# State-space tiles: one decay matrix for both directions, time steps in the scans, the gate on GpSimd

## The reference

```python
def segsum_exp(a):   # out[..., i, j] = exp(sum_{k=j+1..i} a[..., k]) for i >= j, else 0
...
Lmat = segsum_exp(A)
Y_diag = jnp.einsum('bcln,bcsn,bhcls,bcshp->bclhp', C, B, Lmat, x)     # x is xh * dt
decay_states = jnp.exp(A_cs[..., -1:] - A_cs)
states = jnp.einsum('bcln,bhcl,bclhp->bchpn', B, decay_states, x)
...
Y_off = jnp.einsum('bcln,bchpn,bhcl->bclhp', C, states, jnp.exp(A_cs))
Y = (Y_diag + Y_off).reshape(b, L, h, p)
...
y = jnp.concatenate([jnp.zeros_like(y[:, :1]), y[:, :-1]], axis=1)
y_fw, y_bw = (y[:b], jnp.flip(y[b:], 1))
fd = x_og @ fc_D_w.T + D
y = y_fw + y_bw + x_og * jnp.repeat(fd, HEADDIM, axis=-1)
yg = y * silu(z)
yn = yg * jax.lax.rsqrt(jnp.mean(yg * yg, axis=-1, keepdims=True) + EPS) * norm_w
return yn @ out_proj_w.T
```

## Time and profile before

| what | us |
|---|---|
| median of 3 runs | 2144.38 (2143.53 to 2150.88) |
| the profiled execution, device time | 2126.43 |
| its span | 2124.7 |
| TensorE busy | 1811.0 (85%) |
| VectorE busy | 1494.5 (70%) |
| ScalarE busy | 1003.0 (47%) |
| GpSimd busy | 447.5 (21%) |

### The profile page before, as it was taken

How to read it: one execution, slowest core, us unless ns; L and a number is a source line. 1 busy time by engine, 2 the same in 40 slices (tenths; PEclk the granted TensorE clock), 3 DMA queues, 4 the chain that set the end, 5 groups by cost and what they waited for, 6 DMA issues and landing times. The chain is left out here.

```text
span 2124.7 us, 33254 instructions
## 1 busy us (share of the span) xinstructions
PE 1811.0 (85%) x10026; PEld 1240.0 (58%) x10026; DVE 1494.5 (70%) x3126; ACT 1003.0 (47%) x2291; POOL 447.5 (21%) x411
## 2 busy tenths in 40 slices
PE   5288898898898969999945695899999898989897
PEld 2146656666666559999942253464656465646564
DVE  5668878788788761222236696878887879888885
ACT  2032242241331412212202254878797979787886
POOL 2113413314314232522111202020111102020101
PEclk9589999899898989999977797999999999999998
DMA  4501221221122119755445294143443424343311
GB/s 161 181 32 60 88 70 59 77 81 59 59 70 88 50 68 320 257 187 179 139 131 175 75 300 135 51 101 69 100 89 86 95 68 102 81 90 80 80 31 31
DMA packets 143788, 226.09 MB, mean 106 GB/s; under 512 B 17725, under 2 KB 110015, under 8 KB 143648
## 3 DMA queue, kind: packets, MB, share of 16 engines
q1 hardware_dynamic: 124464, 179.95, 27.6%
q0 software_dynamic: 19184, 44.45, 8.3%
HBM read 174.26 MB, written 50.99 MB: 106 GB/s over the span
## 5 line engine op out<-in xcount | busy, mean ns | idle before, releaser
L2239 DVE TENSOR_SCALAR att_scores<-att_psS 128x512 f32<-128x512 f32 x512 | 348.7, 681 | 74.7 <-PE att_psS L2073 60.0
L2188 ACT ACTIVATE att_prob<-att_scores,att_shift 128x512 f32<-128x512 f32 x512 | 383.3, 749 | 30.3 <-DVE att_shift L2255 30.3
L2197 ACT COPY att_pT<-att_psT 128x512 f32<-128x512 f32 x512 | 305.7, 598 | 140.3 <-PE att_psT L2081 139.9
L2081 PEld LDWEIGHTS att_psT<-ident,att_prob 128*128 128x128 f32 x2048 | 244.7, 142 | 176.9 <-issue 78.4
L2247 DVE CUSTOM_DVE_ANT_0 att_scores<-att_scores,first_decay 128x512 f32<-128x512 f32 x512 | 347.6, 679 | 0.0
L2081 PE MATMUL att_psT<-ident,att_prob 128*128 128x128 f32 x2048 | 317.0, 278 | 26.6 <-ACT att_pT L2197 26.0
L2073 PE MATMUL att_psS<-first_ks,first_qs 128*128 128x512 bf16 x512 | 197.5, 387 | 33.5 <-DVE att_scores L2239 29.4
L2095 PE MATMUL att_psO<-att_pT,att_v 128*32 128x512 f32 x1024 | 139.6, 620 | 24.5 <-ACT att_pT L2197 24.5
L1233 DVE TENSOR_TENSOR_SCAN mamba_L<-mamba_am,mamba_begin 128x1024 f32<-128x1024 f32 x64 | 145.5, 2295 | 15.0 <-PE mamba_psY L954 14.7
L1460 PEld LDWEIGHTS ffn_psH<-ffn_xT,ffn_w 128*128 128x128 f32 x1248 | 147.3, 194 | 3.6 <-issue 1.7
L1460 PE MATMUL ffn_psH<-ffn_xT,ffn_w 128*128 128x128 f32 x1248 | 147.7, 277 | 1.1 <-ACT ffn_xT L1494 1.1
(11 more groups left out here) (282 smaller groups left out, 2916.7 us busy)
## 6 DMA issues: line engine op xcount, KB each, us to landing
ffn_w<-in_w SPq DMA_DIRECT2D x39, 1024.0 KB, 5.1
mamba_am<-a_rows SPq DMA_DIRECT2D x64, 512.0 KB, 3.7
first_qs<-q_parts SPq DMA_DIRECT2D x256, 64.0 KB
first_ks<-k_parts SPq DMA_DIRECT2D x256, 64.0 KB
xn<-xn_all SPq DMA_DIRECT2D x16, 512.0 KB, 5.8
ffn_w<-in_w POOLq DMA_DIRECT2D x8, 1024.0 KB, 6.2
att_w<-in_inter POOLq DMA_DIRECT2D x7, 1024.0 KB, 6.1
att_w<-in_outer POOLq DMA_DIRECT2D x7, 1024.0 KB, 7.2
```

The source lines that it names most:

```text
L2081: mm = nc.tensor.transpose(ps[:, k * P:(k + 1) * P], prob[:, n % NP, k * P:(k + 1) * P], C.ident[:])
L2188: nc.scalar.activation(prob[:, n % NP], scores[:, n % NCL], ACT.Exp, bias=shift[:, h % 2, t:t + 1], accum_out=total[:, octet % 2, t, j, i: ...
L2197: nc.scalar.copy(pT[:, h % HEADS_T, :, t * P:(t + 1) * P], bank_of("turn", n)[:].rearrange("p (k q) -> p k q", k=CPB)).then_inc(pT_ready, 1)
L2239: vec.tensor_scalar(scores[:, n % NCL], psS[n % NS][:], -CLAMP, CLAMP, ALU.max, ALU.min).then_inc(clipped, 1)
```

## The change

In the third part the two directions of a tile share one matrix. A scan's `begin` now holds the time step of the row's token and direction instead of 1, so that `xdt` isn't needed and the diagonal product takes `xl` itself. Since the forward matrix is 0 above the diagonal of the shifted tile and the backward one below, GpSimd adds the two (`join`), VectorE picks for every place the product of its direction (`choose`: by masks `side`, then a sum of both halves into `pair`), multiplies once per tile (`decays`), and TensorE's diagonal product runs once per tile. `begin` is made anew for each unit by a select of GpSimd (`beginnings`) in the memory of the table's `hot_row`, four buffers. The gate's multiplication moves from VectorE's `finish` to GpSimd (`gate`). Four scans instead of three stand ahead of `dtdec`, and VectorE's and TensorE's loops go over tiles instead of units. The diff, cut to its core (the declarations, semaphores and renamed counts of waits are left out):

```diff
-    NA, NL = 4, 3
+    NA, NM, NB = 4, 3, 4
...
+        begin = table.hot_row[:].rearrange("p k (b h) t -> p (k b) h t", b=NB)
... (TensorE)
-                    def diagonal(u):
-                        t, d = u // 2, u % 2
-                        if d == 0:
...
-                        pe.wait_ge(L_ready, i * U + u + 1)
-                        pe.wait_ge(xdt_ready, i * U + u + 1)
+                    def diagonal(t):
...
+                        pe.wait_ge(L_ready, i * CPB + t + 1)
                         for h in range(NH):
-                            mm = nc.tensor.matmul(psY[:, h * HD:(h + 1) * HD], L[:, u % NL, h], xdt[:, u % 2, h * HD:(h + 1) * HD],
+                            mm = nc.tensor.matmul(psY[:, h * HD:(h + 1) * HD], fwd[:, t % NM, h], xl[:, t, h * HD:(h + 1) * HD],
...
+                    def from_states(t):
+                        for d in range(2):
+                            if (d == 0 and t > 0) or (d == 1 and t < CPB - 1):
+                                pe.wait_ge(state_ready, (i + 1) * 6)
+                                done = [2 * (t - 1) if t > 1 else 0, 2 * t][d]
+                                pe.wait_ge(off_scaled, i * 6 + done)
...
-                    diagonal(0)
-                    for u in range(2, U + 1):
-                        if u % 2 == 0 and 4 <= u < U:
-                            products(u // 2)
-                        diagonal(u - 1)
-                        if u in (4, 6):
-                            turn_tile(u // 2 - 2)
-                            output(u // 2 - 2)
+                    for t in range(CPB):
+                        diagonal(t)
+                        from_states(t)
+                        if t + 2 < CPB:
+                            products(t + 2)
+                        if 1 <= t < CPB - 1:
+                            turn_tile(t - 1)
+                            output(t - 1)
... (GpSimd)
+                    def beginnings(t):
+                        pool.wait_ge(decayed, i * U + max(2 * t + 2 - NB, 0))
+                        nc.gpsimd.tensor_tensor(turn[:, t:t + 1], C.ones[:, 0:1], C.ones[:, 0:1], ALU.mult)
+                        for d in range(2):
+                            u = 2 * t + d
+                            side_of = 1 - 2 * d
+                            nc.gpsimd.affine_select(out=begin[:, u % NB], in_=dtb[:, d, t].unsqueeze(2).to_broadcast([P, NH, P]),
+                                                    compare_op=ALU.is_equal, fill=0.0, base=-1,
+                                                    pattern=[[0, NH], [side_of, P]], channel_multiplier=-side_of).then_inc(begin_ready, 1)
+                    def gate(t):
+                        pool.wait_ge(z_ready, (i + 1) * CPB)
+                        pool.wait_ge(summed, i * CPB + t + 1)
+                        nc.gpsimd.tensor_tensor(y[:, t % 2], y[:, t % 2], zs[:, t], ALU.mult).then_inc(gated, 1)
+                    def join(t):
+                        pool.wait_ge(decayed, i * U + 2 * t + 2)
+                        nc.gpsimd.tensor_tensor(fwd[:, t % NM], fwd[:, t % NM], bwd[:, t % 2], ALU.add).then_inc(joined, 1)
+                    pool.wait_ge(ab_ready, i + 1)
+                    beginnings(0)
+                    beginnings(1)
+                    join(0)
... (VectorE)
+                    def choose(t):
+                        dve.wait_ge(g_ready, i * CPB + t + 1)
+                        v.tensor_tensor(masked[:], gT[t % 2], side[:], ALU.mult).then_inc(sided, 1)
+                        dve.wait_ge(sided, i * CPB + t + 1)
+                        c.step(v.tensor_tensor(pair[:, t % 2], masked[:, 0], masked[:, 1], ALU.add))
+                    def decays(t):
+                        dve.wait_ge(joined, i * CPB + t + 1)
+                        v.tensor_tensor(fwd[:, t % NM], fwd[:, t % NM], pair[:, t % 2].unsqueeze(1).to_broadcast([P, NH, P]), ALU.mult).then_inc(L_ready, 1)
...
-                        dve.wait_ge(summed, i * CPB + t + 1)
-                        v.tensor_tensor(y[:, b], y[:, b], zs[:, t], ALU.mult).then_inc(gated, 1)
...
+                    choose(0)
                     decays(0)
                     grow(0)
-                    decays(1)
+                    choose(1)
                     grow(1)
                     grow(2)
+                    decays(1)
...
+                    for t in range(CPB):
+                        if 1 <= t and t + 1 < CPB:
+                            choose(t + 1)
+                            decays(t + 1)
+                        for d in range(2):
+                            count = off(t, d, count)
+                        finish(t)
+                        if t + 2 < CPB:
+                            products_of(2 * t + 4)
+                            products_of(2 * t + 5)
+                        if 2 <= t < CPB:
+                            outputs(t - 2)
```

More of the change, by code:

```diff
@@ L704, in mamba @@
         am = s.sb("am", [P, NA, 1 + NH * P + 1])
-        begin = s.sb("begin", [P, 2, NH, P])
-        L = s.sb("L", [P, NL, NH, P])
-        xdt = s.sb("xdt", [P, 2, DI])
+        fwd = s.sb("fwd", [P, NM, NH, P])
+        bwd = s.sb("bwd", [P, 2, NH, P])
+        side = s.sb("side", [P, 2, P])
+        masked = s.sb("masked", [P, 2, P])
+        pair = s.sb("pair", [P, 2, P])
+        turn = s.sb("turn", [P, CPB])
         xfd = s.sb("xfd", [P, 2, DI])
@@ L933, in products @@
                     def products(t):
-                        pe.wait_ge(L_ready, i * U + (2 * t - 2 if t >= 2 else 0))
+                        pe.wait_ge(sided, i * CPB + (t - 1 if t >= 2 else 0))
                         for e in range(2):
@@ L956, in diagonal @@
                         mm.then_inc(diag_used, 1)
-                        if (d == 0 and t > 0) or (d == 1 and t < CPB - 1):
-                            pe.wait_ge(state_ready, (i + 1) * 6)
-                            done = [2 * (t - 1) if t > 1 else 0, 2 * t][d]
-                            pe.wait_ge(off_scaled, i * 6 + done)
-                            lo = t * P + (0 if d == 0 else 2)
-                            nc.tensor.matmul(psO[d][:], xc[:, 5 + 2 * d, lo:lo + P], state[:, d, t],
-                                             start=True, stop=True).then_inc(off_ready, 1)
+                    def from_states(t):
[4 more added lines that the diff above has]
+                                pe.wait_ge(off_scaled, i * 6 + done)
+                                lo = t * P + (0 if d == 0 else 2)
+                                nc.tensor.matmul(psO[d][:], xc[:, 5 + 2 * d, lo:lo + P], state[:, d, t],
+                                                 start=True, stop=True).then_inc(off_ready, 1)
@@ L1182, in _ @@
                     table.rows_hot(nc, dve, choice, 0, q)
+                v.tensor_copy(side[:, 0], C.before[:]).then_inc(mask_made, 1)
+                v.tensor_copy(side[:, 1], C.after[:]).then_inc(mask_made, 1)
+                dve.wait_ge(mask_made, 2)
                 dve.wait_ge(conv_in, 3 * 16)
                 def own_weights():
-                    dve.wait_ge(begun, 3)
                     dve.wait_ge(weights_in, 5 * 16)
@@ L1232, in products_of @@
                         back = -1 if d else 1
-                        v.tensor_tensor_scan(L[:, u % NL].rearrange("p h t -> p (h t)")[:, ::back],
+                        to = bwd[:, t % 2] if d else fwd[:, t % NM]
+                        v.tensor_tensor_scan(to.rearrange("p h t -> p (h t)")[:, ::back],
                                              am[:, u % NA, at:at + NH * P][:, ::back],
-                                             begin[:, d].rearrange("p h t -> p (h t)")[:, ::back], 0.0,
+                                             begin[:, u % NB].rearrange("p h t -> p (h t)")[:, ::back], 0.0,
                                              ALU.mult, ALU.add).then_inc(decayed, 1)
-                    for u in range(NL):
+                    for u in range(4):
                         products_of(u)
```

92 lines of the change are left out of this document (39 added, 53 removed).

## The result

The changed kernel takes **2264 us** (median; 2269 in a second set of runs) against 2145 for the one before: a ratio of 1.0538, 95% interval 1.0506 to 1.0569, and 1.0569 [1.052, 1.0618] in the second set. It is about 120 us slower. The forecast was 2234 with a range of 2165 to 2272. One execution of the first set (3870 us) was slow from start to end and is left out, so the profile shown here is one of the second set, of the same kernel.

The account below looks back on a forecast made before the run. VectorE was taken to set the pace after the state updates. Per sequence, 6.9 us saved, 18.8 of new waits replacing 2.6, and 1.9 for low clock gave +11.2; eight sequences, 90, made 2234 us, range 2165 to 2272.

Parts of the forecast that it names:

- states end: End of a sequence's state updates, counted from its first copy: forecast at 47.1 us, against 47.0 in the kernel before.
- 1 join 1: After the state updates, VectorE's multiplication for tile 1 waits for GpSimd's `xfd`, `turn`, two selects and join: 3.7 us.
- 2 `xfd` first; y + yo: GpSimd's queued `xfd` takes SBUF ahead of VectorE, 1.0 us; then the first y + yo meets a select, 1.2 us.
- 3 two scans held up by gates: Gates of tiles 0 and 1 ask during a scan and hold up the next one: 0.85 us each.
- 4 joins 2 and 3: VectorE's next big step waits for GpSimd's joins of tiles 2 and 3: 2.4 and 2.7 us.
- 5 two round trips: TensorE's second state product of tiles 1 and 2 waits for VectorE's reader: 2.3 us, plus 1.9 at half clock.
- 6 last state product: At the sequence's end VectorE waits for TensorE's turn, output, D part, diagonal and state product: 3.8 us.
- The first rival: TensorE's clock stays low from the second wait to the last state product: 5.1 us a sequence, 2275 us; chance 0.22.
- Work taken from VectorE behind 47.0 is worth its full time: After the state updates (47.0 us into a sequence) VectorE sets the pace, so its reduced work counts fully: 6.9 us.
- second rival: GpSimd's operations fall in VectorE's free moments and the clock stays up: +3.3 us a sequence, 2171 us; chance 0.20.
- the other side: TensorE's tail is covered by VectorE's join wait, races won, joins fast: -3.1 us a sequence, 2119 us; faster 0.06.
- term (b): Multiplications by the products after the state updates fall from six to three: 3.4 us less VectorE work a sequence.

Follow-up runs that it names:

- e2: The changed kernel with GpSimd's join of tile 1 put ahead of the first `xfd` and of the selects for tile 2: 2263.8 us, ratio 1.0551.
- e3: The changed kernel with the gate's multiplication back in VectorE's `finish`, all else as changed: 2264.9 us, ratio 1.0558.
- e5: e4 with the scans of tiles 2 and 3 ahead of `off` and `finish`, and GpSimd's joins as early as inputs allow: 2161.4 us, ratio 1.0086.
- e4: Changed kernel; TensorE's second state product waits only for its own buffer's reader, VectorE's first output step precedes tile 3's multiplication: 2193.4 us, ratio 1.0228.
- b2: The kernel before with only the gate's multiplication moved from VectorE to GpSimd: 2143.2 us, ratio 0.9996.
- b6: b3 with the later scans left where the kernel before has them, so only the fourth scan moves ahead: 2125.1 us, ratio 0.9923.
- b1: The kernel before with four buffers of L, a fourth scan ahead and each later scan one unit earlier: 2164.1 us, ratio 1.0097.
- b3: b1 with TensorE's second state product waiting only for the last reader of its own buffer: 2159.4 us, ratio 1.0067.
- b4: The kernel before with only TensorE's second state product waiting for its own buffer's last reader: 2144.6 us, ratio 1.0005.

## Why the prediction was right, and where it was not

The side and the range were right (2264 and 2269, near its upper end of 2272), and so was the mechanism: GpSimd holds up VectorE, VectorE holds up TensorE, and the new waits exceed the work saved. Of the difference of about 120, 90 were forecast. Its steps, for a sequence, forecast against the rows above:

| step | forecast | measured |
|---|---|---|
| states end | 47.1 | 48.6 |
| 1 join 1 | 3.7 | 3.66 |
| 2 `xfd` first; y + yo | 1.0 + 1.2 | 0.85 + 0.75 |
| 3 two scans held up by gates | 0.85 + 0.85 | 1.01 + 1.01 |
| 4 joins 2 and 3 (`choose` and its multiplication beyond their own 0.25 or 0.29 and 1.20) | 2.4 + 2.7 | 2.7 + 2.9 |
| 5 two round trips (forecast: 2.3 for both, 1.9 for the half clock; measured: the first, the second) | 2.3 + 1.9 | 2.23 + 1.68 |
| 6 last state product | 3.8 | **8.57** |

The left column behind the states adds up to 20.7, the right one to 25.4; VectorE's own work came out as forecast. 4.7 from the table and 1.5 from the states make 6.2 more than the 11.2 forecast, against the 82.05 that the sum was made from (99.0 - 82.05 = 16.95; 0.4 less of own work makes up the rest).

**Steps 1 to 5** were read rightly, each within 0.5. One holder of SBUF at a time, and whoever has asked longer next: that gives the gate's 3.18, the scans' 3.29, and both `pair` rows. But they were written down as separate costs, as if each could be taken away, and e2 shows that they can't: with step 1 gone, the states ended later and step 4 grew, together by as much. That the holding time of both engines is what bounds them together fits e2 and e3, but wasn't tried by itself; e5 shows that another order of the same work takes 32 us off. The join took 2.34 rather than the 2.08 chosen, inside the bounds; by the Trainium skill ("GPSIMD Engine Reference", section 3.1), which gives 4497 ns for 2048 columns, half of that is an estimate of 2.25. There the Trainium skill's figure was nearer than the row of 512 columns taken twice, and should have been chosen.

**Step 6 is the term that was mis-sized**: 3.8 for 8.57, which is most of the miss. Two things were left out. The turn, output, D part and diagonal product of this path were costed at the full clock, and ran largely at the lower one (the output 3.78 for 1.97, the D part 1.92 for 1.05, the turn 1.06 for 0.60, the diagonal 2.28 for 1.90: 3.5 in all). And the output of tile 1 waits for VectorE's first output step, which stands behind `finish(2)`: 2.37 where 0.77 of copying had been allowed for, 1.6 more. That is a circle: second product, `yo`, `finish(2)`, output step, output, D part, product, `yo`. Of these 5.1, 4.8 showed up as waiting. e4 loosens this circle and takes 34 us.

**The first rival was nearer than the forecast.** Low clock to the sequence's end gave 2275, at a chance of 0.22; the measured 2264 to 2269 lie closer to it than to 2234. Its mechanism did act, with a break at 582 to 588, and it began earlier than either text has it: at 558, in TensorE's wait of 4.61 for the sums of tile 0, ahead of the round trips. That the rival's sum fits so well is in part luck: of its 5.1 for step 6 the clock gave 3.5, and the wait for the output step, which it didn't have, 1.6. The reason held against it, a mean clock of 0.96 in the sequence of the earlier trace rows, came from one sequence of the short kind; three of six in the same trace stood at 0.90, which a look at the windows of all eight would have shown. The Trainium skill ("TensorE: Matmul & The Clock Gate", section "HAM oscillation — how this bites in real kernels") says that waits between bursts throttle the clock repeatedly, and the trace agrees: the clock is at 0.50 behind the wait of 4.61 in all eight sequences, and the stage's mean granted clock (130 to 790) is 0.78 after against 0.93 before. The miss on the states' end belongs here as well: the first two `xdd` ended only 0.3 later than forecast (37.8), but behind them TensorE's eight passes for the states took 3.77 and 2.75 with the clock at 0.50 up to about 548, where they had taken 2.92 and 2.02 in the kernel before. That is 1.6 us, and the miss was 1.5.

**"Work taken from VectorE behind 47.0 is worth its full time" was wrong.** It counted -6.9 a sequence. b2 takes 2.8 of it alone and gains nothing; b6 takes 2.3 and keeps 0.7 of it; b1, the same scan with the others moved too, gains nothing even in sequences where the clock stays up. TensorE follows so closely that VectorE's waits of 2.64 showed who came last, and not by how much. In the kernel after this error is hidden, since the waits were counted step by step; it would have made any milder version of this change look like a gain. The second rival (races won, 2171) and the other side (2119) didn't occur: VectorE and GpSimd met in nearly every step. The sign given for GpSimd, some 40 us busy a sequence, came out as 47.6, because its standing still counts as busy, too.

What stays open: the split of step 6 between clock and order is worked out from rows; e4 changes the order and leaves the clock low for the output, but no edit keeps the clock up with the circle in place. No run took the combined multiplications (term (b)) alone. With order mended, the change as a whole is still 0.7 to 0.9% slower than the kernel before.

## What to carry to other kernels

Where two engines hand work to each other with waits of 1 or 2 us, what one of them is relieved of isn't won: cost it on both, and try it alone before adding it to a sum. When order moves across queues, follow each chain through every shared buffer until it meets itself, and look at the granted clock of every repetition, not of one. Work given to GpSimd was paid by VectorE here wherever both read SBUF; look for a place for it beside VectorE's work on PSUM.

## What the runs showed of the hardware

- The clock has two outcomes for one and the same program. A wait of 1.99 us in front of the D part of tile 1 was followed by a granted clock of 0.50 in the sequence of the earlier trace rows and of 1.00 in the next. Over all sequences of before, b1, b2, b3, b4 and b6, the clock fell behind this wait in 0 of 8 with 1.38 us, 0 of 2 with 1.57, 15 of 24 with 1.99 or 2.00, 2 of 2 with 2.51 and 10 of 12 with 2.94; the two exceptions are in b1, at 253 and 335. So no single length of the wait parts the two outcomes here. Between b3 and b6 the work is the same and only the places of scans differ; the wait is 1.56 us shorter, and the kernel is 34 us (1.6%) faster.
- The low clock lasted from 558 to 582 in the kernel after, though TensorE was busy without a break in parts of it (562 to 564 above).
- An unblocked gate on GpSimd took 1.26, longer than the 1.02 of an `xdd` of the same 512 columns, whose second input is one factor per head. Both were costed alike.
- Two selects of 1024 columns took 2.13 unblocked, 1.07 each, below the 1.28 that stood in the trace of before.
- A VectorE copy of 32 columns, with one input, in SBUF, is held up as well: 1.07 for 0.17 beside a gate on GpSimd (603.80 in the kernel after).
